# Norm stage of a pre-norm transformer block: scaling moved to GpSimd, first weights split earlier, last residual moved into attention

## The reference

```python
def layernorm(x): return (x - mean(x)) / sqrt(var(x) + 1e-5)
def attn(x):                       # x is already layer-normed
    y = x * rsqrt(mean(x*x) + 1e-6) * rms_w
    q, k, v = split(y @ w_in.T)    # 32 query heads in 8 groups, 8 key and 8 value heads, 64 wide
    q, k = rope(q), rope(k)
    o = causal_softmax(q @ k.T / 8) @ v
    return x + o @ w_out.T
def ffn(x):                        # ternary weights: mean(|W|) * clip(round(W / mean(|W|)), -1, 1)
    return x + (silu(x @ Wg.T) * (x @ Wu.T)) @ Wd.T
x = x + attn(layernorm(x))
x = x + ffn(layernorm(x))
```

## Time and profile before

| | |
|---|---|
| median of 3 runs | 1977.03 us (1976.73 to 1977.76) |
| the profiled execution, its own time | 1976.19 us |
| its span, first to last instruction | 1974.4 us |
| PE, POOL, DVE, ACT busy | 97%, 72%, 62%, 48% of the span |
| `normalise` | from 0 to about 42 us of the span |
| `attention` | from 43 to about 1453 us |
| mean granted TensorE clock | 0.994 |

### The profile page before, as it was taken

One profiled execution on the slowest core, in us unless ns is written; L12 is line 12 of the kernel. 1 busy time (PEld: TensorE's weight loads), 2 busy tenths in 40 slices (PEclk: granted clock), 3 DMA queues, 4 the chain that ended last, 5 costly groups with the idle time before them and its releaser, 6 DMA issues. The chain is left out here.

```text
span 1974.4 us, 55173 instructions
## 1 busy us (share of the span) xinstructions
PE 1917.4 (97%) x21382; PEld 1183.2 (60%) x21382; DVE 1233.7 (62%) x3283; ACT 938.5 (48%) x1997; POOL 1424.5 (72%) x1627
## 2 busy tenths in 40 slices
PE   4999999999999999999999999999999998999999
PEld 3566666666666666666666666666654443444444
DVE  7787588668767876876886687687735652121221
ACT  4465566556555665655556566556732202121110
POOL 2799999999999999999999999999940002131221
PEclk9999999999999999999999999999999999999999
DMA  6332242244215224421522332244156510000000
GB/s 212 68 79 40 53 95 55 51 81 84 54 33 116 51 49 84 74 50 42 107 49 45 72 70 47 40 90 93 37 174 213 211 66 1 17 5 21 5 16 22
DMA packets 301812, 136.79 MB, mean 69 GB/s; under 512 B 248576, under 2 KB 285696, under 8 KB 300032
## 3 DMA queue, kind: packets, MB, share of 16 engines
q1 hardware_dynamic: 301568, 133.43, 30.1%
HBM read 49.48 MB, written 25.17 MB: 38 GB/s over the span
## 5 line engine op out<-in xcount | busy, mean ns | idle before, releaser
L816 POOL TENSOR_TENSOR pl<-p 128x512 f16<-128x512 f32 (+3 forms) x1280 | 1138.8, 920 | 38.0 <-ACT p L655 35.0
L655 ACT ACTIVATE p<-a_ps 128x512 f32<-128x512 f32 (+3 forms) x1280 | 678.2, 533 | 552.4 <-PE a_ps L588 329.9
L731 DVE TENSOR_REDUCE mpart<-a_ps 128x1 f32<-128x512 f32 x768 | 508.7, 686 | 131.5 <-PE a_ps L572 126.9
L604 PE MATMUL a_ps<-v,p 128*128 128x65 f16 x4352 | 527.6, 193 | 6.3 <-POOL pl L816 5.7
L606 PE MATMUL a_ps<-v,p 128*128 128x64 f16 x4352 | 530.1, 194 | 0.0
L608 PE MATMUL a_ps<-v,pl 128*128 128x65 f16 x4352 | 526.9, 192 | 0.0
L604 PEld LDWEIGHTS a_ps<-v,p 128*128 128x128 bf16 x4352 | 412.4, 97 | 110.0 <-issue 8.4
L606 PEld LDWEIGHTS a_ps<-v,p 128*128 128x128 bf16 x4352 | 405.8, 97 | 108.0
L588 PE MATMUL a_ps<-q_lm,k_h 128*128 128x512 f16 (+3 forms) x1280 | 444.4, 347 | 0.0
L587 PE MATMUL a_ps<-q_hh,k_hl 128*128 128x512 f16 (+3 forms) x1280 | 443.5, 347 | 0.0
L572 PE MATMUL a_ps<-k_hl,q_hh 128*128 128x512 f16 (+3 forms) x1280 | 428.8, 348 | 8.9 <-issue 5.8
(11 more groups left out here) (101 smaller groups left out, 2280.0 us busy)
## 6 DMA issues: line engine op xcount, KB each, us to landing
yh<-attn_scratch SPq DMA_DIRECT2D x32, 512.0 KB, 4.4
raw<-ffn_t SPq DMA_DIRECT2D x12, 1024.0 KB, 4.9
attn_scratch<-o_turn SPq DMA_DIRECT2D x32, 256.0 KB, 3.1
attn_scratch<-o_turn_late SPq DMA_DIRECT2D x32, 256.0 KB, 3.2
wraw<-w_in_t SPq DMA_DIRECT2D x8, 768.0 KB, 5.1
resid_scratch<-raw SPq DMA_DIRECT2D x4, 1024.0 KB, 4.5
raw<-w_out_t SPq DMA_DIRECT2D x16, 256.0 KB, 3.6
x<-resid_scratch SPq DMA_DIRECT2D x4, 1024.0 KB, 7.7
```

Source lines behind the costliest of these rows:

```text
L604: nc.tensor.matmul(o, weights, v[:, par, j, 0:VU], start=(j == 0 and t == 0), stop=False, skip_group_check=True)
L655: nc.scalar.activation(p32[:, i % RING, r * P:CHUNK], sbank(i)[:, r * P:CHUNK], ACT.Exp, scale=SCALE).then_inc(exp_done, 1)
L731: nc.vector.reduce_max(mpart[:, u % 2, t, kk:kk + 1], bank, AX.X).then_inc(maxs_used, 1)
L816: nc.gpsimd.tensor_tensor(pl[:, i % RING, cols], p32[:, i % RING, cols], p_high[:, i % RING, cols], ALU.subtract).then_inc(low_ready, 1)
```

## The change

Three things are changed. In `normalise`, the first chunk is scaled by DVE as before, and chunks two to four by POOL, each after its `inv`. The first input weights are loaded after the second chunk of `x` instead of after the fourth; ACT splits them after the second chunk's residual, DVE after the third chunk's low parts. And the last chunk's residual is left out of `normalise`: ACT makes it at the beginning of `attention`, and SP stores it there tile by tile, behind the four attention stores of group 0. For that `zcoef` has a place for each chunk, and it and the semaphore are passed on.

```diff
@@ sync
             for c in range(1, NCH):
                 sp.dma_start(xin[:, tiles(c), :], x_v[:, tiles(c), :]).then_inc(x_in[c], 16)
-            for to, source in ahead[1:3]:
-                sp.dma_start(to, source).then_inc(w_in, 16)
+                if c == 1:
+                    for to, source in ahead[1:3]:
+                        sp.dma_start(to, source).then_inc(w_in, 16)
-            for b in range(NCH):
+            for b in range(NCH - 1):
                 sp.wait_ge(z_ready, TPC * (b + 1))
                 sp.dma_start(r_v[:, tiles(b), :], xin[:, tiles(b), :]).then_inc(z_out, 16)
@@ vector
+            statistics(0)
+            scaled()
+            for b in range(NCH):
+                residual_coefficients(b)
+                if b < NCH - 1:
+                    statistics(b + 1)
                 if b == 1:
                     dve.wait_ge(w_in, 32)
                     nc.vector.tensor_scalar(wscale[:, :], wscale[:, :], W_SCALE, None, ALU.mult).then_inc(scale_ready, 1)
+                low_parts(b)
+                if b == 2:
+                    for kt in range(KT):
+                        dve.wait_ge(w_high, kt + 1)
+                        nc.vector.scalar_tensor_tensor(wl[:, kt, :], wraw[:, kt, :], wscale[:, kt:kt + 1], wh[:, kt, :], ALU.mult,
+                                                       ALU.subtract)
@@ gpsimd
                 nc.gpsimd.tensor_tensor(inv[:, b % 2], veps[:, b % 2], mhalf[:, :, :], ALU.pow).then_inc(inv_ready, 1)
+                if b:
+                    pool.wait_ge(inv_ready, b + 1)
+                    for t in range(TPC):
+                        pool.wait_ge(yt_ready, TPC * (b - 1) + t + 1)
+                        nc.gpsimd.tensor_scalar(y[:, t, :], xin[:, b * TPC + t, :], mv[:, b % 2, t, 0:1], inv[:, b % 2, 0, t:t + 1],
+                                                ALU.subtract, ALU.mult).then_inc(y_ready, 1)
@@ scalar, normalise
                 if b < NCH - 1:
-                    residual(b)
-                else:
+                    act.wait_ge(z_coef, b + 1)
+                    residual(nc, xin, zcoef, b, z_ready)
+                if b == 1:
                     act.wait_ge(scale_ready, 1)
                     for kt in range(KT):
                         nc.scalar.activation(wh[:, kt, :], wraw[:, kt, :], ACT.Copy, scale=wscale[:, kt:kt + 1]).then_inc(w_high, 1)
-                    residual(b)
@@ attention, sync and scalar
+            def store_residual(n):
+                sp.wait_ge(z_ready, n - (TT - TPC) + 1)
+                sp.dma_start(resid_dram[n * P:(n + 1) * P, :], raw[:, n * D:(n + 1) * D]).then_inc(z_out, 16)
...
+                    if kind == "store" and g == 0:
+                        store_residual(TT - TPC + c)
...
+            act.wait_ge(z_coef, NCH)
+            residual(nc, raw.rearrange("p (n d) -> p n d", d=D), zcoef, NCH - 1, z_ready)
             act.wait_ge(ones_set, 2)
```

More of the change, by code:

```diff
@@ L52, with residual, normalise @@
 Late = namedtuple("Late", "o_hl o_turn o_turned o_stored")
-def normalise(nc, x, resid_dram, xin, yh, yl, wraw, wh, wl, wscale, ident, ahead, z_out):
+def residual(nc, xin, zcoef, b, done):
+    for t in range(TPC):
+        n = b * TPC + t
+        nc.scalar.activation(xin[:, n, :], xin[:, n, :], ACT.Identity, scale=zcoef[:, b, 0, t:t + 1],
+                             bias=zcoef[:, b, 1, t:t + 1]).then_inc(done, 1)
+def normalise(nc, x, resid_dram, xin, yh, yl, wraw, wh, wl, wscale, ident, ahead, z_out, zcoef, z_coef):
     x_v = x[0].rearrange("(n p) d -> p n d", p=P)
@@ L81, in normalise @@
         inv_ready = sem("n_inv_ready")
-        z_coef = sem("n_z_coef")
         z_ready = sem("n_z_ready")
@@ L120, in statistics @@
                 dve.wait_ge(stat, TPC * (b + 1))
+                if b >= 2:
+                    dve.wait_ge(y_ready, TPC * (b - 1))
                 for t in range(TPC):
@@ L126, in statistics, with scaled, residual_coefficients, low_parts @@
                 nc.vector.tensor_scalar(veps[:, b % 2, 1].unsqueeze(2), var, LN_EPS, None, ALU.add).then_inc(var_ready, 1)
-            def scaled(b):
-                dve.wait_ge(inv_ready, b + 1)
[L130 to L136, removed]
+            def scaled():
+                dve.wait_ge(inv_ready, 1)
+                for t in range(TPC):
+                    nc.vector.tensor_scalar(y[:, t, :], xin[:, t, :], mv[:, 0, t, 0:1], inv[:, 0, 0, t:t + 1],
+                                            ALU.subtract, ALU.mult).then_inc(y_ready, 1)
+            def residual_coefficients(b):
+                dve.wait_ge(inv_ready, b + 1)
                 mean, rstd = mv[:, b % 2, :, 0:1], inv[:, b % 2, 1].unsqueeze(2)
-                nc.vector.tensor_scalar(zcoef[:, b % 2, 0].unsqueeze(2), rstd, 1.0, None, ALU.add)
-                nc.vector.scalar_tensor_tensor(zcoef[:, b % 2, 1].unsqueeze(2), mean, -1.0, rstd, ALU.mult, ALU.mult)\
+                nc.vector.tensor_scalar(zcoef[:, b, 0].unsqueeze(2), rstd, 1.0, None, ALU.add)
+                nc.vector.scalar_tensor_tensor(zcoef[:, b, 1].unsqueeze(2), mean, -1.0, rstd, ALU.mult, ALU.mult)\
                     .then_inc(z_coef, 1)
[L142 to L146, removed]
+            def low_parts(b):
                 for t in range(TPC):
@@ L347, with attention @@
 W_OUT_WIDTH = CT * D // W_OUT_PARTS
-def attention(nc, w_in_t, w_out_t, attn_dram, yh, yl, consts, cos, sin, wraw, wh, wl, wscale, raw, z_out, late, att_in):
+def attention(nc, w_in_t, w_out_t, attn_dram, yh, yl, consts, cos, sin, wraw, wh, wl, wscale, raw, z_out, zcoef, z_coef, resid_dram, late, att_in):
     w_v = w_in_t.rearrange("g (k p) n -> p g k n", p=P)
@@ L393, in attention @@
         misc_ready = sem("misc_ready")
+        z_ready = sem("z_ready")
         rope_parts = sem("rope_parts")
@@ L1275, in build @@
             z_out = ctx.enter_context(nc.semaphore("z_out"))
+            z_coef = ctx.enter_context(nc.semaphore("z_coef"))
+            zcoef = sb("zcoef", [P, NCH, 2, TPC], F32)
             consts = sb("consts", [P, 4, P], F16)
@@ L1289, in build @@
             xin = raw[:, :].rearrange("p (n d) -> p n d", d=D)
-            normalise(nc, x, resid, xin, yh, yl, wraw, wh, wl, wscale, ident, ahead, z_out)
-            attention(nc, w_in_t, w_out_t, attn, yh, yl, consts, cos, sin, wraw, wh, wl, wscale, raw[:, :], z_out, late, att_in)
+            normalise(nc, x, resid, xin, yh, yl, wraw, wh, wl, wscale, ident, ahead, z_out, zcoef, z_coef)
+            attention(nc, w_in_t, w_out_t, attn, yh, yl, consts, cos, sin, wraw, wh, wl, wscale, raw[:, :], z_out, zcoef, z_coef, resid,
+                      late, att_in)
         with ExitStack() as ctx:
```

7 lines of the change are left out of this document (1 added, 6 removed).

## The result

The changed kernel takes 1983.94 us at the median (1980.71 to 1986.09, 6 runs), the kernel before 1977.57 in the same batch (1976.73 to 1981.45, 6 runs): ratio 1.0031, 95% interval 1.0021 to 1.0042. It is 6.4 us slower, past the bound of 0.2%; the forecast was 3.7 us faster. Its profiled execution took 1982.86 with a span of 1980.9. That is 6.7 more than the profiled execution of before (1976.19), and PE is again busy for 97% of the span.

The account below looks back on a forecast made before the run. PE, busy 97% of the span, sets the time, and DVE bounds a round of `normalise`. Midway between B and C, (2.9 + 4.4) / 2 = 3.7 us off the median 1977.03 gave 1973.3; range 1969.6 to 1978.0.

Parts of the forecast that it names:

- The scaling on POOL: In `normalise`, 12 scalings of length T, taken as 0.9 us each, between 0.57 and 1.38.
- The rival with that mechanism: POOL's scaling bounds `normalise` and the kernel is slower; 1982.2 us at T = 1.9, chance 0.12.
- My break-even: Scaling length on POOL at which, with strict turns, PE starts no earlier than before: 1.26 us.
- Waits between DVE and POOL: In `normalise`, DVE's coefficients, variances and `wl` were expected to wait beside POOL's scalings; `wl` in attention waits 0.35 us, 0.83 at most.
- B: `normalise` with DVE and POOL in strict turns, T = 0.9: PE starts at 40.2, 2.9 us earlier.
- C: `normalise` with DVE waits of 0.35 us each, T = 0.9: PE starts at 38.6, 4.4 us earlier.
- A: `normalise` without DVE-POOL waits, T = 0.9: PE starts at 36.7, 6.4 us earlier; as a rival 1970.6, chance 0.22.
- Removed from the end: Last residual and `wh` leave ACT's tail, four `wl` DVE's; `normalise` ends at 37.66, 4.1 us earlier.
- The residual in attention: The last residual's 2.91 us on ACT at the start of attention, hidden before the ropes' copies; cost 0.
- the four stores: Residual stores in group 0, each one issue ahead of `q_lm` or `q_hh` transposes on SP; cost 0, 2 us if seen.
- the loads: Last two chunks of `x` land later, behind 768 KB of weights, with covers of 2.3 us and more; cost 0.
- The clock: PE's clock at the first projections, half rate there costing 2.0 us; change counted 0, ends -2.0 and +1.5.

Follow-up runs that it names:

- two_inputs: The changed kernel with POOL adding each fp32 tile to itself in place of scaling it; 1975.26 us (1 run; kernel before 1976.9).
- one_op: The changed kernel with the subtraction of the mean left out of POOL's scaling; 1979.6 us (1 run; kernel before 1977.48).
- share2_fill: The changed kernel with DVE scaling two tiles of each later chunk, POOL two, and `wl` ahead of the last low parts; 1974.22 us, ratio 0.9985.
- scale_only: The changed kernel with weights and last residual back where they were, only POOL's scaling kept; 1986.5 us, ratio 1.0046.
- weights_only: The kernel before with only the first input weights loaded and split early; 1977.04 us, ratio 1.0004.
- dve_scale: The changed kernel with all scalings given back to DVE, early weights and late residual kept; 1973.54 us, ratio 0.9984.
- share2_warm: share2_fill with 16 unread matmuls added in PE's idle stretches of the last two chunks of `normalise`; 1975.46 us, ratio 0.9990.
- share2_again: share2_fill run a second time, unchanged; 1973.85 us, ratio 0.9981.
- share2_load: share2_fill with group 1's weight load issued behind the third chunk's key transposes in group 0; 1975.6 us, ratio 0.9991.

## Why the prediction was wrong

**The step that failed** is "The scaling on POOL: 12 operations of a length T", by its upper bound. I took T = 0.9 and let it end at 1.38, arguing that a scaling has one input fewer than an addition and must be cheaper. It took 2.06. The two rows from which I scaled were two-input additions, and two_inputs shows that they were fair for their own kind (1.01 for 512 columns, 1.09 at the mean with its hold-ups; 1.38 in proportion was even too high). The kind of instruction decides, not the number of inputs: two operations with a scalar for each partition cost twice an addition with two full inputs. The rule of the Trainium skill that I set beside it (GPSIMD Engine Reference, Engine selection: one-input operations at roughly line rate) would have put T near 0.5; by the trace a one-operation scaling takes 1.55 and this one 4.3 times what DVE needs, so it doesn't hold here. What did point the right way stood in my own rival: `pow` on eight elements takes 1.65 us, so POOL is dear where its arithmetic is.

**The rival with that mechanism is what happened**, at a chance of 0.12, with a total of 1982.2 at T = 1.9. Its sum comes near (stage end by its formula 38.9 + 8 x 1.16 = 48.2, found 47.9), but for another reason. It had eight T on the path and DVE and POOL in strict turns. In the trace all twelve stand in a row, with almost no turns: 14.77, three `pow` at 1.65 with their starts at 0.1, twelve T at 2.06, 0.67 for `wl` and 2.53 for transposes, copy and low part. That is 47.9. From the same chain the change breaks even where the first projection is again at 43.07, 5.6 us down from 48.66: at T = 2.06 - 5.6 / 12 = 1.60. one_op ran at 1.55 and started at 43.19, with its first `pow` 0.7 us later than in the change, which agrees. My break-even was 1.26.

**Waits between DVE and POOL** were mispriced in the other direction. B (strict turns) and C (0.35 each) both put them on DVE. In the change `wl` takes 2.19 for four, as before (2.20), and of the small operations some grew, by 0.14 to 0.44 us (`zcoef` at 39.38: 0.59 against 0.15), and some not at all; none of it was on POOL's path. It is POOL that was held up, by 0.67 us beside `wl`, and by 0.93 in share2_fill. The rows of single instructions show when: in each of the nine profiles with `wl` beside POOL's scalings, a scaling (in two_inputs an addition) that had begun ahead of the first `wl` kept its length, though up to three `wl` began beside it, and one that began while a `wl` was running took 0.16 to 0.94 us more (in the change the one at 38.52, with a `wl` from 38.24 to 38.85). The last of the four `wl` was held up too in six of them, by some 0.36 us (0.96 or 0.97 instead of 0.61), and in two_inputs the first three were (0.86, 1.39 and 1.39). The strict lock that the Trainium skill describes (SBUF — State Buffer, Who interferes with whom) would have made a `wl`, or the second coefficient, both with two inputs in SBUF, wait for the end of the scaling under way, up to 2 us; no row of this stage shows it (the longest hold-up of DVE beside a 2.06 us scaling is 0.47, `zcoef` in share2_fill at 31.47). A was nearly right here, and would have been the forecast with T known.

**Removed from the end.** 4.1 us by the prediction. In scale_only the last engine leaves 4.1 us (51.34, ACT's residual) behind the last low part (47.22), in the change none. Right. The barrier behind the last engine was 1.31 us only when ACT is last (41.76 to 43.07; 42.05 to 43.35 in weights_only); where DVE is last it is 0.75 (47.90 to 48.66, 39.76 to 40.51). I had used 1.31 throughout, 0.55 too much wherever DVE is last.

**The residual in attention, the four stores and the loads** at nothing: right. ACT still waits 3.78 us behind the residual, no DVE row waits for a load (one small slip: 768 KB at 2.7 us for 1024 KB is 2.0 us, not 2.1), and groups are as full as before. dve_scale, in which these parts are alone, is faster by 3.9 us.

**The clock** at nothing: nearly. In the change projections are 0.32 us apart from 48.66 to 53.5 and 0.16 after it, so 4.8 us at half against 4.0 before: 0.4 us more.

**What stays open.** Of share2's 4.7 us at the start only 2.7 to 2.9 arrive in the total at the medians, and the traces tell where to look. Counted from the first projection, the 481st exponential (the first of the fourth group) comes 2.3 to 6.2 us later than before in the four profiles of the shared kernels (6.2 in share2_warm, whose profiled execution was the slowest of its eleven), but between 0.9 us earlier and 0.8 later in the nine other profiles. One of these is two_inputs, whose projections start just as early (38.58). So most of the loss arises in the first three groups, and an early start alone doesn't bring it. In the profiled executions the stretches at half clock fall otherwise each time (share2_again has one at 420.7, share2_load one at 1370.9, before none at either), each worth up to 1.7 us, and the same group takes up to 2 us more or less from one execution to another (the third, between share2_fill and share2_again, which are one kernel). Neither warming PE nor moving the load recovered the rest, and what takes it isn't settled. Also not shown: by what mechanism a scaling that begins beside a `wl` is held up and one under way is not.

## What to carry to other kernels

A price for an operation on an engine that has not run it is bounded only by rows of the same kind of instruction (same class, same number of arithmetic steps, same kind of operands); where there is none, the range must reach to a multiple, and the first question is from which price on the engine becomes the stage's chain. Before work is moved off the busiest engine of a stage, write down the new chain of the one that receives it, all its instructions in a row: here 1.75 + 4 T a chunk against a round of 7.4. Where two engines leave a stage together, taken off one alone the work brings little (0 and 1.9 us), off both 2.6. If the scaling is to be shared, then by halves; all of it on DVE with the two other moves gave as much (0.9984 against 0.9985 and 0.9981) and is the simpler kernel.

## What the runs showed of the hardware

- POOL on fp32 tiles of 128 x 512: two operations with scalars for each partition 2.06 us, with constants 1.90, one operation 1.55, an addition with two inputs (the same tile twice) 1.01; the first on 256 columns 1.21. DVE does the first in 0.48.
- A scaling on POOL that begins while a `wl` runs on DVE takes longer (2.74 instead of 2.07 us in the change, 3.01 in share2_fill, 2.19 instead of 1.57 in one_op), and one that has begun ahead of the `wl` does not. `wl` keeps its 0.61 us in most cases; the last of a row of four took 0.96 or 0.97 in six profiles.
- The clock can fall to half while PE is at work: in share2_warm at 35.43, as a run of 2.30 us of matmuls began right behind four transposes, and in dve_scale at 41.1, with projections under way. Both times it had been at full ahead of it.
